# A Macaron transformer block on one core: another order of the Q, K and V projections, Q copied by halves, output projection in quarters

## The reference

```
x = x + 0.5 * ffn(layernorm(x))        # ffn: silu(gate) * up, 1376 wide, 4-bit weights, dequantised
x = x + attention(layernorm(x))        # 32 heads of 16, one K and one V head shared, ALiBi, causal softmax
x = x + 0.5 * ffn(layernorm(x))        # the same weights
```

## Time and profile before

| what | value |
|---|---|
| median of 3 runs | 673.7 us (673.36 to 674.21) |
| the profiled execution's own time | 672.25 us |
| its span, first to last instruction | 670.2 us |
| PE, DVE, ACT, POOL busy | 575.2, 327.3, 159.2, 89.0 us |
| mean granted TensorE clock | 0.936 |
| attention phases 0 to 3, first shifted score to FFN pass 2 | 256.5 to 473.9 us |

### The profile page before, as it was taken

One profiled execution on the slowest core, in us unless ns is written; L12 is line 12 of the kernel. 1 busy time (PEld: TensorE's weight loads), 2 busy tenths in 40 slices (PEclk: granted clock), 3 DMA queues, 4 the chain that ended last, 5 costly groups with the idle time before them and its releaser, 6 DMA issues.

```text
span 670.2 us, 7580 instructions
## 1 busy us (share of the span) xinstructions
PE 575.2 (86%) x2968; PEld 413.3 (62%) x2968; DVE 327.3 (49%) x647; ACT 159.2 (24%) x286; POOL 89.0 (13%) x113
## 2 busy tenths in 40 slices
PE   1499999999999996890599479678899999999998
PEld 1387777788886773550364134233668887788886
DVE  6798999573114446571256356566321133511113
ACT  1333332221111112331123233444201111211111
POOL 5675000003100001121012111231000000000000
PEclk9999999999999997895689779969799999999999
DMA  7579110591592800009203800000097000100001
GB/s 211 164 234 308 43 41 17 131 431 65 131 152 32 94 1 4 1 1 163 30 1 95 98 1 1 5 1 1 0 268 218 1 1 0 64 0 1 1 0 63
DMA packets 37195, 51.52 MB, mean 77 GB/s; under 512 B 10188, under 2 KB 27702, under 8 KB 36760
## 3 DMA queue, kind: packets, MB, share of 16 engines
q1 hardware_dynamic: 32320, 40.13, 25.3%
q0 software_dynamic: 2656, 10.57, 4.7%
q10 hardware_dynamic: 2184, 0.35, 0.5%
HBM read 35.82 MB, written 15.02 MB: 76 GB/s over the span
## 4 chain that ended last, share of the span: by engine, by line
PE 58%; DVE 6%; DMA 5%; ACT 3%; issue 1%; SPq 0%; ACTq 0%; DVEq 0%
PE bank L1324 23%; PE bank L1342 11%; PE bank L1481 4%; PE bank L1407 4%; PE bank L1374 3%; PE bank L1453 3%; PE bank L1399 3%; DMA qp_c<-q_rows 2%; DVE nm L1086 2%; PE bank L1439 2%; PE bank L1474 2%; DMA qp_c<-two 1%; PE bank L1294 1%; PE bank L1355 1%; DVE x L925 1%
## 5 line engine op out<-in xcount | busy, mean ns | idle before, releaser
L1342 PE MATMUL bank<-w_d,hs 128*128 128x512 f32 (+1 forms) x528 | 129.1, 394 | 2.6 <-DVE hs L916 1.3
L1342 PEld LDWEIGHTS bank<-w_d,hs 128*128 128x128 f32 (+1 forms) x528 | 98.0, 188 | 26.3 <-issue 3.8
L910 DVE TENSOR_TENSOR hf<-sil,bank 128x512 f32<-128x512 f32 (+1 forms) x44 | 30.2, 686 | 162.8 <-PE bank L1324 162.7
L1086 DVE TENSOR_REDUCE nm<-bank 128x2 f32<-128x512 f32 (+1 forms) x96 | 61.8, 685 | 93.6 <-PE bank L1407 93.6
L1324 PE MATMUL bank<-xt,w_far 128*128 128x512 f32 (+1 forms) x384 | 92.5, 394 | 0.0
L1324 PE MATMUL bank<-xt,w_mid 128*128 128x512 f32 x384 | 90.1, 390 | 0.0
L1324 PE MATMUL bank<-xt,w_near 128*128 128x512 f32 x288 | 73.4, 412 | 9.4 <-issue 9.4
L1324 PEld LDWEIGHTS bank<-xt,w_mid 128*128 128x128 f32 x384 | 72.0, 188 | 14.9
L1324 PEld LDWEIGHTS bank<-xt,w_far 128*128 128x128 f32 (+1 forms) x384 | 69.3, 181 | 18.2
L1324 PEld LDWEIGHTS bank<-xt,w_near 128*128 128x128 f32 x288 | 56.5, 199 | 23.5 <-issue 10.8
L628 ACT ACTIVATE sil<-bank 128x512 f32<-128x512 f32 (+1 forms) x44 | 26.2, 597 | 141.4 <-PE bank L1324 141.2
(11 more groups left out here) (148 smaller groups left out, 588.9 us busy)
## 6 DMA issues: line engine op xcount, KB each, us to landing
gate_up_part<-w_mid SPq DMA_DIRECT2D x1, 4096.0 KB, 15.3
q_rows<-qst SPq DMA_DIRECT2D x8, 512.0 KB, 4.4
w_mid<-gate_up_part SPq DMA_DIRECT2D x4, 1024.0 KB, 9.2
gate_up_part<-w_far SPq DMA_DIRECT2D x1, 3840.0 KB, 23.9
qp_a<-q_rows SPq DMA_DIRECT2D x12, 256.0 KB, 11.3
w_far<-gate_up_part SPq DMA_DIRECT2D x3, 1024.0 KB, 8.9
raw_d<-in_L_ffn_qweight_down SPq DMA_DIRECT2D x10, 256.0 KB
x<-in_L_attn_hidden_states SPq DMA_DIRECT2D x8, 256.0 KB, 3.6
```

The lines of the kernel that those rows point to most:

```text
L910: nc.vector.tensor_tensor(hf[0:jw(jt(s, p)), n % 2, :], sil[0:jw(jt(s, p)), n % 2, :], up_ps[0:jw(jt(s, p)), :], ALU.mult).then_inc(h_ok, 1)
L1086: nc.vector.tensor_reduce(nm[:, min(u, 1), 2 * h0 + s:2 * (h0 + heads) + s - 1:2], bank[6 + s][:, :].rearrange("p (h n) -> p h n", h=heads ...
L1342: ins = nc.tensor.matmul(acc[t][:, :], hs[0:jw(j), n % 2, a, t * P:(t + 1) * P], w_d[0:jw(j), j, b, :], start=(p == 0 and q == 0), stop=(p ...
```

## The change

`constant_rows` reads only the constants; `q_to_dram` and `q_to_rows` take one half h at a time (two DMAs of 256 KB, six of 128 KB), so a sequence has 14 landings instead of 8. For sequence 2, Q is projected at steps 4 to 7 of phase 0 and K and V at step 8. For sequence 3, transposes move to phase 0, step 9, Q to steps 10 and 11 of phase 0 and 0 and 1 of phase 1, K and V to step 2 of phase 1. The output projection goes by quarters: steps 5, 8, 9, 9, 10, 10, 11, 11 in phases 1 and 2, and 4, 4, 5, 5, 6, 6, 8, 8 in phase 3. The maxima are split at step 9 and sent at step 10. `scores(1, 0)` and `scores(1, 1)` stand ahead of and behind the last `down` of FFN pass 1, and phase 0 takes units 2 to 11.

The diff, its lines moved left by eight columns and unchanged lines partly left out:

```diff
@@ -282,7 +282,9 @@
 def score_units(b, n):
-    return [] if b >= B else range(NU)[4 * n // 3:4 * (n + 1) // 3]
+    first = 2 + n if b == 1 else 4 * n // 3
+    count = 1 + (n == 8) if b == 1 else 1 + (n % 3 == 2)
+    return [] if b >= B or n > 8 else range(first, first + count)
 def ln_bank(b, t):
@@ -404,38 +406,52 @@
...
-    def q_to_dram(b):
-        sp.wait_ge(a_qhi, 2 * b + 2)
-        sp.wait_ge(a_qlo, 2 * b + 2)
-        for part in range(2):
-            sp.dma_start(q_rows[b, part], qst[:, part, :, :].bitcast(F32).rearrange("p m q -> p (m q)"))\
-                .then_inc(q_out[b], 16)
-    def q_to_rows(b):
+    def constant_rows(b):
...
             sp.dma_start(dst[64 * s + 16:64 * s + 32, :], slope_rows[s]).then_inc(q_in[b], 16)
-        sp.wait_ge(q_out[b], 32)
+    def q_to_dram(b, h):
+        sp.wait_ge(a_qhi, 2 * b + h + 1)
+        sp.wait_ge(a_qlo, 2 * b + h + 1)
+        for part in range(2):
+            sp.dma_start(q_rows[b, part, :, 2 * h * S:2 * (h + 1) * S],
+                         qst[:, part, 2 * h:2 * h + 2, :].bitcast(F32).rearrange("p m q -> p (m q)"))\
+                .then_inc(q_out[b], 16)
+    def q_to_rows(b, h):
+        sp.wait_ge(q_out[b], 64 if b == 1 else 32 * (h + 1))
+        dst = qp[b][:, :, :].bitcast(F32).rearrange("p (o m) q -> p o (m q)", o=NO)
         for s in range(2):
             for row0, part in ((0, 0), (32, 1), (48, 0)):
-                src = bass.AP(q_rows.tensor, ((2 * b + part) * P + HD * s) * KT * S,
-                              [[KT * S, HD], [2 * HD * KT * S, NO], [1, KT * S]])
-                rows = dst[64 * s + row0:64 * s + row0 + HD, :].rearrange("p (o f) -> p o f", o=NO)
+                src = bass.AP(q_rows.tensor, ((2 * b + part) * P + HD * s) * KT * S + 2 * h * S,
+                              [[KT * S, HD], [2 * HD * KT * S, NO], [1, 2 * S]])
+                rows = dst[64 * s + row0:64 * s + row0 + HD, :, 2 * h * S:2 * (h + 1) * S]
                 sp.dma_start(rows, src).then_inc(q_in[b], 16)
-    q_to_dram(0)
-    q_to_rows(0)
-    q_to_dram(1)
+    constant_rows(0)
+    for h in range(2):
+        q_to_dram(0, h)
+        q_to_rows(0, h)
+    q_to_dram(1, 0)
+    q_to_dram(1, 1)
     sp.wait_ge(up_ok, NJ + 8)
-    q_to_rows(1)
+    constant_rows(1)
+    q_to_rows(1, 0)
+    q_to_rows(1, 1)
     sp.wait_ge(up_ok, 2 * NJ)
-    q_to_dram(2)
-    q_to_rows(2)
+    constant_rows(2)
+    for h in range(2):
+        q_to_dram(2, h)
+        q_to_rows(2, h)
     sp.wait_ge(a_st, 2 * NU)
-    q_to_dram(3)
-    q_to_rows(3)
+    constant_rows(3)
+    for h in range(2):
+        q_to_dram(3, h)
+        q_to_rows(3, h)
     sp.wait_ge(a_st, 2 * NU * B)
...
@@ -654,7 +670,7 @@
...
         if b >= 1 and h == 0:
-            act.wait_ge(q_out[b - 1], 32)
+            act.wait_ge(q_out[b - 1], 64)
         src = q_bank(b, h)[:, :].rearrange("p (m q) -> p m q", m=2)
...
@@ -669,7 +685,7 @@
...
         act.wait_ge(a_mlo, b + 1)
-        act.wait_ge(q_in[b], 16 * 8)
+        act.wait_ge(q_in[b], 16 * 14)
         for s in range(2):
...
@@ -751,18 +767,18 @@
-        if b in (0, 1):
-            at = 4 if b == 0 else 1
-            if n == at:
-                x_copy(b + 2, 0)
-                x_copy(b + 2, 1)
-            if n == at + 1:
-                k_high(b + 2)
-            if n in (at + 3, at + 5):
-                q_high(b + 2, (n - at - 3) // 2)
+        if (b, n) in ((0, 3), (0, 9)):
+            x_copy(2 + (n == 9), 0)
+            x_copy(2 + (n == 9), 1)
+        if (b, n) in ((0, 5), (0, 7), (0, 11)):
+            q_high(2 + (n == 11), int(n == 7))
+        if (b, n) == (1, 1):
+            q_high(3, 1)
+        if (b, n) in ((0, 8), (1, 2)):
+            k_high(b + 2)
+        if n == 9 and b + 1 < B:
+            max_high(b + 1)
         if n == 10 and b + 1 < B:
-            max_high(b + 1)
-        if n == 11 and b + 1 < B:
             max_to_rows(b + 1)
...
@@ -1188,19 +1204,20 @@
...
         units(2)
-        if j == NJ - 1:
-            max_low(0)
+    max_low(0)
+    maxima(1, 0)
+    maxima(1, 1)
     def between(b, n):
-        if b in (0, 1):
-            at = 4 if b == 0 else 1
-            if n == at + 1:
-                k_low(b + 2)
-            if n in (at + 3, at + 5):
-                q_low(b + 2, (n - at - 3) // 2)
+        if (b, n) in ((0, 5), (0, 7), (0, 11)):
+            q_low(2 + (n == 11), int(n == 7))
+        if (b, n) == (1, 1):
+            q_low(3, 1)
+        if (b, n) in ((0, 8), (1, 2)):
+            k_low(b + 2)
         if b == 0:
...
@@ -1215,13 +1232,11 @@
...
                 xn_tile(tile_no("attn", 2, 1), 5)
-            if n == 11:
+            if n == 8:
                 xn_tile(tile_no("attn", 3, 0), 6)
                 xn_tile(tile_no("attn", 3, 1), 7)
-        if b == 1 and n in (9, 11):
-            attn_out(0, (n - 9) // 2)
-        if b >= 2 and n in (7, 9):
-            attn_out(b - 1, (n - 7) // 2)
+        if b >= 1 and n in ((6, 8) if b == B - 1 else (9, 11)):
+            attn_out(b - 1, int(n > 6 if b == B - 1 else n > 9))
         if b == B - 1:
...
@@ -1240,7 +1255,7 @@
...
                     ffn_xn(2, 3)
-        if n == 10 and b + 1 < B:
+        if n == 9 and b + 1 < B:
             max_low(b + 1)
...
@@ -1349,7 +1364,7 @@
     def project_kv(b):
         pe.wait_ge(a_xt, 2 * b + 2)
-        pe.wait_ge(*((a_qlo, 1), (a_qlo, 3), (a_xt, 5), (a_xt, 7))[b])
+        pe.wait_ge(a_qlo, (1, 3, 6, 8)[b])
         ps = kv_bank(b)
...
@@ -1366,9 +1381,9 @@
...
             pe.wait_ge(a_xt, 2 * b + 2)
-            if h == 1 and b >= 1:
-                pe.wait_ge(a_kp, b + (b >= 2))
-                pe.wait_ge(a_vp, 2 * (b + (b >= 2)))
+            if h == 1 and b == 1:
+                pe.wait_ge(a_kp, b)
+                pe.wait_ge(a_vp, 2 * b)
         for n in steps:
...
@@ -1382,7 +1397,7 @@
...
         if k == 0:
-            pe.wait_ge(q_in[b], 128)
+            pe.wait_ge(q_in[b], 16 * 14)
             pe.wait_ge(a_kp, b + 1)
...
@@ -1487,23 +1502,34 @@
-        if b in (0, 1):
-            at = 3 if b == 0 else 0
-            if n == at:
-                pe.wait_ge(*((x_upd, 8) if b == 0 else (a_qlo, 6)))
-                for t in range(2):
-                    transposes(tile_no("attn", b + 2, t), ln_bank(b + 2, t))
-            if n == at + 1:
-                project_kv(b + 2)
-            if n in range(at + 2, at + 6):
-                h, half = divmod(n - at - 2, 2)
-                project_q(b + 2, h, range(4 * half, 4 * half + 4))
-        first = 7 if b == 1 else 5
-        if b >= 1 and n in range(first, first + 4):
-            t, half = divmod(n - first, 2)
-            if half == 0:
-                pe.wait_ge(*((a_qlo, 7 + t) if b == 1 else (a_x, 2 * b - 2)))
-            project_out(b - 1, t, range(2 * half, 2 * half + 2))
+        if (b, n) in ((0, 3), (0, 9)):
+            if n == 3:
+                pe.wait_ge(x_upd, 8)
+            else:
+                pe.wait_ge(a_qlo, 6)
+                pe.wait_ge(a_kp, 3)
+                pe.wait_ge(a_vp, 6)
+            for t in range(2):
+                transposes(tile_no("attn", 2 + (n == 9), t), ln_bank(2, t))
+        if b == 0 and n in (4, 5, 6, 7):
+            h, half = divmod(n - 4, 2)
+            project_q(2, h, range(4 * half, 4 * half + 4))
+        if (b, n) in ((0, 10), (0, 11), (1, 0), (1, 1)):
+            h, half = b, n % 2
+            project_q(3, h, range(4 * half, 4 * half + 4))
+        if (b, n) in ((0, 8), (1, 2)):
+            project_kv(b + 2)
+        if b >= 1:
+            quarters = (4, 4, 5, 5, 6, 6, 8, 8) if b == B - 1 else (5, 8, 9, 9, 10, 10, 11, 11)
+            for q, step in enumerate(quarters):
+                if step == n:
+                    t, k = divmod(q, 4)
+                    if k == 0 and b == 1:
+                        pe.wait_ge(*((a_kp, 4) if t else (a_qlo, 7)))
+                        pe.wait_ge(a_vp, 8 * t)
+                    if k == 0 and b >= 2:
+                        pe.wait_ge(a_x, 2 * b - 2)
+                    project_out(b - 1, t, range(k, k + 1))
         if b == B - 1 and n in (7, 9):
...
@@ -1566,15 +1592,14 @@
...
             max_transposes(0)
+    scores(1, 0)
     down(1, NJ - 1)
+    scores(1, 1)
...
         for n in range(NU):
-            if (b, n) == (0, 0):
-                for k in score_units(1, 0):
-                    scores(1, k)
             shifted_scores(b, n)
-            units = score_units(b + 1, n) if (b, n) != (0, 0) else ()
+            units = score_units(b + 1, n)
             for k in units[0:1]:
...
```

## The result

| | before | changed |
|---|---|---|
| median | 673.91 us (4 runs, 673.36 to 674.21) | 639.1 us (4 runs, 638.51 to 639.81) |
| profiled execution, its span | 672.25, 670.2 us | 639.81, 638.1 us |
| mean granted TensorE clock | 0.936 | 0.967 |

The account below looks back on a forecast made before the run. It took four TensorE gaps, together 38.1 us, waiting for maxima and Q's head rows, as the bound. 27.8 + 5.4 + 4.1 + 1.3 - 1.3 - 1.0 - 1.5 = 34.8 us won gave 637.5 profiled, 639 median; range 631 to 653.

Parts of the forecast that it names:

- 7, phase 3: Phase 3, 40.3 us before: quarters and `attn_out` one step earlier, start no longer cold; 1.3 us won.
- Part 1: Before phase 0: sequence 0's Q copied by halves, with a new wait in `q_high(1, 0)`; 1.3 us lost.
- Part 2: Start of phase 0: scores ahead of `down`, `ffn_out` 4 us later, transposes 1.5 us later; 1.0 us lost.
- Part 3: Phase 0: 51.5 us instead of 55.6, maxima contending with reads of sequence 2's Q; 4.1 us won.
- Part 4: Phase 1: the 11.67 us gap for sequence 2's head rows goes; sequence 2's constants meet only maxima with time to spare.
- Part 5: Phase 1: 46.5 us instead of 74.3, the 10.82 us gap before phase 2 gone; 27.8 us won.
- Part 6: Phase 2: 41.8 us instead of 47.2, three groups of 10.5 and one of 10.3; 5.4 us won.
- steps don't close up: Phases 1 and 2: removed work had only filled waits for maxima, so groups stay at 12.7 us; 652 us, 20%.
- Part 8: Q copies: time goes by bytes, 7 us a half; 1.5 us charged for it being up to 8.5.
- the rival of 14 us a half: Q copies: time goes by pieces, so sequences 0 and 2 come late; 665 us, 7%.
- the way to a slower kernel: Q copies: four halves on the path, each us over 7 costing about 4; slower at 15.7 us a half, 3%.
- the signs named in advance: Phases 0 to 3: TensorE idles, maxima landings, phase lengths, clock 1.00 and head-row rates that would confirm or refute the forecast.

Follow-up runs that it names:

- the uncovered transposes of the maxima: Changed kernel with the output projection in halves at the old steps: 649.44 us, ratio 0.9641.
- order: Changed kernel with Q copied whole, maxima one step later and output projection in halves, leaving the new order of projections: 659.07 us, ratio 0.9812.

## Why the prediction was right

It was right in direction, in mechanism for the three large gaps, and in the place of most of the gain: 26.1 of 33.8 us are in phase 1. The experiments show the mechanism and not only the gaps: whole copies bring back the landing of 9.2 us, late maxima bring back gaps before phases 2 and 3, the uncovered transposes of the maxima bring back 4.33.

That the number agreed to 0.1 us is luck. The forecast in the profiled execution's terms was 637.5 us, and that execution took 639.81, 32.4 us less than before's; the medians are 34.8 apart because the profiled execution lies 1.7 us under its median before and 0.7 over it now. Its terms against the trace:

| term | said | measured |
|---|---|---|
| 1 and 2, before phase 0 | -2.3 | -0.35 |
| 3, phase 0 | +4.1 | +1.2 |
| 5, phase 1 | +27.8 | +26.1 |
| 6, phase 2 | +5.4 | +4.3 |
| 7, phase 3 | +1.3 | +2.5 |
| 8, size of the copies | -1.5 | in the others |

- **Part 1** held to the order of events: the new wait came, for 4.38 us, where I had put it. But the last of the four writes landed by 193.03, not at 195.8, and the wait ended ahead of the next silu.
- **Part 2**: `ffn_out` came 3.9 us later (260.43 against 256.49), as said, but the transposes of sequence 2 only 0.1 us later after the first shifted score, where I had 1.5.
- **Part 3** is the one that went wrong. I had the maxima held up by the reads of half 1, until 307.5. Those were issued by 297.6 and land 4.2 us after issue. What held them was the constants of sequence 3, which part 3 did not count though the diff moves them: SP is free to read them at a_st = 24, in the middle of the maxima's way. The amount was too small as well. I had some 2 us for contention (51.5 against the bound of 49.6 without any); the run with the constants held took 49.8 and 49.0 us, so it cost 4.6 to 5.4, and phase 0 took 54.4.
- **Part 4** held: no gap for head rows, the constants of sequence 2 harmless.
- **Part 5**: groups of 10.4 and 10.0, and 9.3 for the last, against 10.5, 10.5 and 10.3: good. The first took 18.5 and not 15.2, for it starts behind the gap that was left: a mean of 0.79 is, by the two levels, an estimated 7.8 us at 1.2 GHz. With the gap gone the whole phase takes 44.6.
- **Part 6**: 9.7, 12.5, 11.3 and 9.4 against 10.5 three times and 10.3. The length that the rival "steps don't close up" gives, 12.7, came in one group, but not its reason: it had TensorE waiting for maxima, and TensorE stood idle 1.7 of those 12.5 us, against 2.4 of the 10.4 in phase 1. With the same work it was busy 10.8 us and not 8.0; what makes the difference is the clock.
- **Part 8**: bytes, not pieces. At the 133 GB/s of its window the 0.79 MB of half 0 take 5.9 us, by this estimate, where I charged up to 8.5, and the rival of 14 us a half is out, with it the way to a slower kernel. The estimate of 109 GB/s by the Trainium skill (SBUF — State Buffer, Door 1: The DMA port swizzle) is passed by 22%; its order of size holds. The rule of large transfers in the Trainium skill (DMA: Bandwidth & Descriptors, Measured) would have had the halves cost something. They cost nothing that a run shows: undone in the changed kernel they are worth 3.4 us, and on the kernel before, with the constants early, 19.5.

Of the signs named in advance, the lengths held (phase 1 48.2, phase 2 42.8, both together 91.0 and not over 95, phase 0 not over 57), and so did the landing of the maxima before phases 2 and 3 (medians of 2.2 and 2.1 us); before phase 1 it was 2.4 to 6.7 us where 4 to 8 was said. Three failed: 5.49 us of idle before L1454 where none over 4 was to be, a clock of 0.79, 0.73 and 0.85 in three groups where 1.00 was to be, and 133 GB/s where 100 to 120 was. The wait around 196 was to be over 3 us for a miss: it was 4.38 us on ScalarE, and TensorE did not wait for it.

The parts are not additive from the kernel before: order 14.9, halves (with early constants) 19.5, quarters 2.5, early maxima -2.0 alone; from the changed kernel backwards 3.4 for halves, 6.8 for maxima, 8.2 for quarters. Order and halves, by these numbers, do much the same job; maxima and quarters have little to cover until those two have cleared the way. That the plain total of the singles is 35.0, against 34.1, is a coincidence of these two.

What stays open is why the clock falls in group two of phase 2 (0.73) with no idle of more than 1.4 us ahead, and not in phase 1 with the same work. What differs is the group ahead of it: steps 0 to 2 of phase 1 hold the projections of sequence 3, those of phase 2 nothing, and from 363.5 to 371.0 TensorE was busy 4.08 of 7.50 us, with the clock down at the end. But the second execution of the changed kernel had a fall in phase 1 too, behind 4.9 busy us in the 6 from 326, so a thin stretch alone doesn't settle it. No kernel tried that.

## What to carry to other kernels

When a buffer is filled through a chain of transfers, start the chain by parts as soon as the first part exists, and then look at what the freed queue does next: the next prefetch, released by the same event, may run into the small transfer that everybody waits for. A wait that holds it back until the small one has landed made the attention phases 7 us shorter here. And judge a cover (work put behind a wait) only in the kernel in which the wait is short enough to be covered: quarters and early maxima, each measured alone, look worth 2.5 us and nothing, and undone one by one in the changed kernel they cost 8.2 and 6.8.

## What the runs showed that I had not expected

- Four DMAs of 16 KB land in 2.1 to 2.3 us (medians) alone, 3.9 (the last 6.7) beside the two DMAs of 256 KB of the constants, and 7.5 to 9.2 beside head rows of 256 KB, with the constants among them in the runs of both ends.
- One DMA issue on ScalarE's queue can take 1.24 us where the median is 0.61; the four together took 3.07, and the activation behind them waited 3.05 us for "issue" at 305.20 above.
- TensorE's granted clock falls to 0.73 on average in the 12.5 us from 369.1. The longest idle ahead of it in the phase is this one:

```profile
368.03 0.60 PE L1414 MATMUL bank<-causal,ident_b 128*128 128x512 bf16 x2 [1.38 <-DVE nm L1102]
```
